# Condition products of tiles 12 to 29 as seven block products a pair

## What is computed

```python
masked_w = weight * mask[None]                       # 8 x 512 x 512
w_bot = einsum('bg,got->bot', y, masked_w)           # one 512 x 512 matrix a batch
h = einsum('bnt,bot->bno', x, w_bot) + bias          # the condition products
gate = silu(bitlinear(h, w_gate)); up = bitlinear(h, w_up)
out = x + bitlinear(gate * up, w_down)
# bitlinear(a, w): a is rounded to 8 bits by its row's largest absolute value,
# w to -1, 0, 1 times the mean of its absolute values
```

## Time and profile before

| | us |
|---|---|
| median of 3 runs | 455.29 |
| lowest, highest | 454.59, 455.42 |
| the profiled execution | 456.14 |
| its span from the first to the last instruction | 454.3 |
| PE busy in it | 436.5 |
| DVE, ACT, POOL busy | 366.3, 326.9, 154.4 |

### The profile page before, as it was taken

The page is one execution under the profiler, slowest core; times in us unless marked ns, Lnnn a source line. Parts: engine busy times, 40 slices in busy tenths (PEclk is TensorE's granted clock), DMA queues, the critical chain, the costliest instruction groups (busy, mean ns, idle before and its releaser), DMA issues.

```text
span 454.3 us, 7179 instructions
## 1 busy us (share of the span) xinstructions
PE 436.5 (96%) x2170; PEld 231.7 (51%) x2170; DVE 366.3 (81%) x624; ACT 326.9 (72%) x448; POOL 154.4 (34%) x160
## 2 busy tenths in 40 slices
PE   4899998999999999999999999999999999999976
PEld 0234443444444455555565556555565555655543
DVE  0316579898956798799998999999999899999971
ACT  1216847785356786988888888888888888888951
POOL 0000170606099554141424414244142432423202
PEclk9999999999999999999999999999999999999989
DMA  7999996995420335253544535344263552635454
GB/s 281 403 399 415 413 249 152 335 278 129 93 48 19 74 71 138 73 115 93 142 81 129 115 83 147 74 135 115 76 155 69 137 119 69 162 66 135 80 139 139
DMA packets 104313, 69.78 MB, mean 154 GB/s; under 512 B 87264, under 2 KB 87264, under 8 KB 102752
## 3 DMA queue, kind: packets, MB, share of 16 engines
q1 hardware_dynamic: 103712, 67.39, 53.8%
q10 hardware_dynamic: 576, 2.10, 1.3%
HBM read 40.11 MB, written 8.39 MB: 107 GB/s over the span
## 4 chain that ended last, share of the span: by engine, by line
PE 77%; DMA 12%; DVE 4%; ACT 3%; issue 2%; SPq 1%; ACTq 0%; DVEq 0%
PE ps L882 24%; PE ps L945 19%; PE ps L917 17%; PE ps L837 10%; DMA wc<-w_gate 4%; PE ps L875 4%; DMA qT<-q_sb 3%; DMA wc<-wcond 2%; DMA wc<-w_down 2%; PE ps L952 2%; PE ps L850 1%; ACT tern_up L406 1%; ACT h_sb L412 1%; DMA wc<-wc 1%; DVE h_max L658 1%
## 5 line engine op out<-in xcount | busy, mean ns | idle before, releaser
L882 PE MATMUL ps<-tern_up,qT 128*128 128x512 f16 x512 | 131.3, 379 | 0.6 <-DVE wc L728 0.6
L837 PE MATMUL ps<-w_bot,xT_sb 128*128 128x512 f32 x256 | 113.2, 595 | 2.3 <-DVE w_bot L633 1.6
L746 DVE TENSOR_REDUCE p_part<-wc 128x1 f32<-128x1536 f32 x64 | 77.9, 1217 | 1.7
L837 PEld LDWEIGHTS ps<-w_bot,xT_sb 128*128 128x128 f32 x256 | 48.0, 190 | 61.2 <-issue 57.5
L882 PEld LDWEIGHTS ps<-tern_up,qT 128*128 (+1 forms) x512 | 50.0, 98 | 55.3 <-DVE wc L728 1.3
L728 DVE TENSOR_TENSOR wc<-ps,xT_sb 128x512 f32<-128x512 f32 x104 | 71.2, 684 | 7.6 <-issue 3.6
L470 ACT ACTIVATE wc<-wc 128x1024 f16<-128x1024 f32 x64 | 66.9, 1051 | 1.8 <-DMA wc<-wc 1.3
L460 ACT ACTIVATE wc<-wc,p_scale 128x2048 f32<-128x2048 f32 x31 | 62.1, 2002 | 4.4 <-DVE p_scale L784 4.4
L945 PE MATMUL ps<-wc 128*128 128x256 f16 x480 | 62.2, 273 | 0.2 <-DVE wc L696 0.2
L696 DVE TENSOR_TENSOR wc<-wc 128x1024 f16<-128x1024 f16 x60 | 56.8, 946 | 3.7 <-DMA wc<-wc 2.5
L455 ACT ACTIVATE xT_sb<-ps,gate_unit 128x512 f32<-128x512 f32 x78 | 49.2, 683 | 11.7 <-PE ps L917 11.3
(11 more groups left out here) (91 smaller groups left out, 544.4 us busy)
## 6 DMA issues: line engine op xcount, KB each, us to landing
xT_sb<-xT SPq DMA_DIRECT2D x32, 256.0 KB, 7.7
x_res<-x SPq DMA_DIRECT2D x30, 256.0 KB, 2.9
out<-result SPq DMA_DIRECT2D x30, 256.0 KB, 2.4
wc<-wcond SPq DMA_DIRECT2D x12, 512.0 KB, 13.7
wc<-w_gate SPq DMA_DIRECT2D x4, 1024.0 KB, 17.7
wc<-w_up SPq DMA_DIRECT2D x4, 1024.0 KB, 13.4
wc<-w_down SPq DMA_DIRECT2D x4, 1024.0 KB, 7.3
wc<-wcond ACTq DMA_DIRECT2D x4, 512.0 KB, 7.6
```

Of the source, the lines that this page charges most:

```text
L746: nc.vector.tensor_reduce(p_part[:, par, i:i + 1], prod[:, par, 512 * lo:512 * hi], AX.X, ALU.max, apply_absolute_value=True).then_inc(par ...
L837: ins = nc.tensor.matmul(ps[:, t % COND_BANKS], xT_sb[:, t % XSLOTS, k], w_bot[:, t // HALF, k], start=(k == 0), stop=(k == KH - 1))
L882: ins = nc.tensor.matmul(ps[:, UP + i % 2], tile_of(s, k), tern_up[:, i, k], start=(k == 0), stop=(k == KH - 1))
```

## The change

- The tiles 12 to 29 become nine pairs r = 6 to 14 (PAIR0 to PAIR_END - 1). Each pair's 2 x 2 output blocks are made by seven products of two k-blocks by 256 columns (pair_product) instead of eight. POOL forms four sums of the tiles' blocks a pair (pair_sum) and, once a batch, four combinations of w_bot's blocks (combine_cond).
- The banks of a pair are 2 (r % 3) and the one after; bank 6 holds the shared block. ACT writes half the bias into a bank ahead of the products (seed_bias) and copies the first product over (copy_first). DVE has pair_share, pair_seed and pair_c22, which add into PSUM, and one pair_largest for both tiles. ACT rounds straight from the bank (pair_round). There is no bias add for these tiles.
- PE's order puts the products 4, 5 and 6 of a pair between those of the next; the last pair's stand beside the first two gate chunks of step 0. Tiles 8 to 11 now use banks 2 to 5. The sums of absolute values stand before tile 9 and in pairs 8 and 12.
- ACT issues the loads of the gate and up weights itself, behind its copies of w_bot and between its first tiles; SP's list of loads is rearranged and the down weight's pieces come with transposes 8 to 11. The x_res loads follow the last transpose.
- The mask of batch 1 moves from DVE to POOL. POOL scales each weight piece between the sums, and DVE cuts a piece as soon as that one is scaled. The last two pieces of the down weight are cut inside step 0. combine_gate(1) follows unit_of(1) and combine_gate(0) follows unit_of(2).
- At the end ACT converts half 0 of tile 30 before copy_seed, SP stores tile 26 before the transposes of tile 30, and tile 31's down products are cut into two halves of 256 columns with a bank, a finish and a store each (down_cut).

The diff, cut to its core (the new functions as far as they carry the order):

```diff
+PLAIN = 12
+PAIR0 = PLAIN // 2
+PAIR_END = LATE // 2
+COND_C = 6
+SUM_TILE = 9
+SUM_PAIR = {8: 1, 12: 2}
+SUM_BANK = (5, 7, 7)
...
+            for t in range(XSLOTS, PLAIN):
+                load_xT(t)
+            transpose_q(0)
+            for t in range(PLAIN, PLAIN + 2):
+                load_xT(t)
+            for k in range(KH):
+                load_mask(1, k)
+            for t in range(1, PAIR0):
                 transpose_q(t)
+                load_xT(PLAIN + 1 + t)
+            for t in range(PAIR0, PLAIN):
+                transpose_q(t)
+                if t == PAIR0:
+                    load_xT(PLAIN + 1 + t)
+                if t >= PLAIN - PIECES:
+                    sp.wait_ge(tern_done, t - PLAIN + PIECES + 1)
+                    load_raw(2, w_down, t - PLAIN + PIECES)
+            for r in range(PAIR0, PAIR_END):
+                for t in (2 * r, 2 * r + 1):
+                    transpose_q(t)
+                for t in (2 * r, 2 * r + 1):
+                    if t + XSLOTS < TILES:
+                        load_xT(t + XSLOTS)
...
+                    pool.wait_ge(x_sum_ready, 4 * n + (0, 1, 0, 2)[i])
+                in0, in1, op = ((a21, a22, ALU.add), (sums[:, 0], a11, ALU.subtract), (a11, a21, ALU.subtract),
+                                (a12, sums[:, 1], ALU.subtract))[i]
+                nc.gpsimd.tensor_tensor(sums[:, i], in0, in1, op).then_inc(x_sum_ready, 1)
...
+            combine_cond(0)
+            for k in range(KH):
+                apply_mask(k)
+            scale_piece(0, 0)
+            scale_piece(0, 1)
+            first_sums(6)
+            last_sums(6)
+            scale_piece(0, 2)
+            scale_piece(0, 3)
+            first_sums(7)
+            last_sums(7)
+            combine_cond(1)
+            first_sums(8)
+            last_sums(8)
+            first_sums(9)
+            scale_piece(1, 0)
+            last_sums(9)
+            scale_piece(1, 1)
+            first_sums(10)
+            scale_piece(1, 2)
+            last_sums(10)
+            scale_piece(1, 3)
+            for r in range(11, 14):
+                first_sums(r)
+                last_sums(r)
+            scale_piece(2, 0)
+            first_sums(14)
+            scale_piece(2, 1)
+            last_sums(14)
+            scale_piece(2, 2)
+            scale_piece(2, 3)
...
+            def seed_bias(r):
+                bank = pair_banks(r)[1]
+                if r < PAIR0 + 3:
+                    act.wait_ge(h_ready, (2, 10, 12)[r - PAIR0])
+                    act.wait_ge(s_bias, 16)
+                else:
+                    act.wait_ge(h_rounded, 2 * r - 5)
+                nc.scalar.activation(ps[:, bank, 0:NB], bias_sb[:, 0:NB], ACT.Copy).then_inc(cond_seeded, 1)
+
+            def copy_first(r):
+                b0, b1 = pair_banks(r)
+                act.wait_ge(cond_first, r - PAIR0 + 1)
+                if r >= PAIR0 + 3:
+                    act.wait_ge(h_rounded, 2 * r - 4)
+                nc.scalar.activation(ps[:, b0, 0:NB], ps[:, b1, 0:NB], ACT.Copy).then_inc(cond_copied, 1)
...
@@ -538,10 +682,10 @@
                     if j is not None:
                         copy_seed(j)
                 else:
+                    if s == TILES - 1:
+                        convert(s - 1, 0, 0)
                     copy_seed(j)
-                    convert(s - 1, 0, 0)
-                if s == TILES - 1:
-                    convert(s - 1, 0, 1)
...
+            for a in range(PIECES):
+                fetch(0, w_gate, a)
+            act.wait_ge(mix_psum, 2 * KH)
             for a in range(PIECES):
                 abs_sum_piece(0, a)
...
+            for a in range(PIECES - 1):
+                cond_round(PIECES + a)
+                abs_sum_piece(1, a)
+            cond_round(7)
+            copy_first(PAIR0)
+            seed_bias(PAIR0 + 1)
+            abs_sum_piece(1, 3)
+            cond_round(8)
+            cond_round(9)
+            copy_first(PAIR0 + 1)
+            cond_round(10)
+            cond_round(11)
+            seed_bias(PAIR0 + 2)
+            for r in range(PAIR0 + 2, PAIR_END):
+                copy_first(r)
+                pair_round(r - 2, 1)
+                if r + 1 < PAIR_END:
+                    seed_bias(r + 1)
+                pair_round(r - 2, 0)
+                pair_convert(r - 2)
+                if 8 <= r < 8 + PIECES:
+                    abs_sum_piece(2, r - 8)
+            pair_round(PAIR_END - 2, 1)
...
                 n = PIECES * m + a
-                dve.wait_ge(scaled, PIECES * (m + 1))
...
+            def pair_share(r):
+                dve.wait_ge(bias_diff_ready, 1)
+                dve.wait_ge(cond_shared, r - PAIR0 + 1)
+                nc.vector.tensor_tensor(pair_shared(r), ps[:, COND_C, 0:NB], bias_diff[:, :], ALU.add
+                                        ).then_inc(cond_shared_out, 1)
+
+            def pair_seed(r):
+                b0, b1 = pair_banks(r)
+                dve.wait_ge(cond_u2, r - PAIR0 + 1)
+                dve.wait_ge(cond_shared_out, r - PAIR0 + 1)
+                nc.vector.tensor_tensor(ps[:, b0, NB:HID], ps[:, b1, 0:NB], pair_shared(r), ALU.add).then_inc(cond_summed, 1)
+
+            def pair_c22(r):
+                b1 = pair_banks(r)[1]
+                dve.wait_ge(cond_u3, r - PAIR0 + 1)
+                dve.wait_ge(cond_shared_out, r - PAIR0 + 1)
+                nc.vector.tensor_tensor(ps[:, b1, NB:HID], ps[:, b1, 0:NB], pair_shared(r), ALU.add).then_inc(cond_c22, 1)
+
+            def pair_largest(r):
+                b0, c = pair_banks(r)[0], 4 + 2 * (r % 2)
+                dve.wait_ge(cond_psum, 2 * r + 2)
+                if r >= PAIR0 + 2:
+                    dve.wait_ge(h_rounded, 2 * r - 2)
...
+            bias_difference()
+            piece_after = {7: 0, 8: 1, 10: 2}
+            for t in range(PLAIN):
                 cond_tile(t)
+                if t == 5:
+                    weight_mean(0)
                 if t in piece_after:
+                    ternary_piece(0, piece_after[t])
+            for r in range(PAIR0, PAIR_END):
+                if r > PAIR0:
+                    pair_seed(r - 1)
+                if r >= PAIR0 + 2:
+                    pair_largest(r - 2)
+                pair_share(r)
+                if r > PAIR0:
+                    pair_c22(r - 1)
+                if r == PAIR0:
+                    ternary_piece(0, 3)
+                if r == 8:
+                    weight_mean(1)
+                if r == 9:
                     units(0)
+                if 10 <= r < 10 + PIECES:
+                    ternary_piece(1, r - 10)
+                if r == 12:
+                    weight_mean(2)
+                if r == 14:
+                    ternary_piece(2, 0)
+            pair_seed(PAIR_END - 1)
+            pair_largest(PAIR_END - 2)
+            pair_c22(PAIR_END - 1)
+            ternary_piece(2, 1)
+            pair_largest(PAIR_END - 1)
...
+                         ps[:, b0, NB:HID], ps[:, b1, 0:NB])[i]
+                for k in range(2):
+                    tile, weight = ((sums[:, 0, k], combos[:, 0, k]), (xT_sb[:, s0, k], w[:, k, 0:NB]),
+                                    (xT_sb[:, s0, 2 + k], w[:, 2 + k, 0:NB]), (sums[:, 1, k], combos[:, 1, k]),
+                                    (sums[:, 2, k], combos[:, 2, k]), (sums[:, 3, k], w[:, 2 + k, NB:HID]),
...
                     pe.wait_ge(half_merged, 2 * KH)
                 else:
+                    pe.wait_ge(h_ready, cond_bank(t) + 1)
...
+                pair_product(r, 1)
+                pair_product(r, 0)
+                if r in SUM_PAIR:
+                    abs_total(SUM_PAIR[r])
+                if r > PAIR0:
+                    pair_product(r - 1, 4)
+                    pair_product(r - 1, 5)
+                pair_product(r, 2)
+                pair_product(r, 3)
+                if r > PAIR0:
+                    pair_product(r - 1, 6)
 
             for s in range(3):
```

318 lines of the change are left out of this document (222 added, 96 removed).

## The result

The changed kernel takes 476.09 us (median of 4 runs, 475.58 to 476.77) beside 454.94 us (454.27 to 455.42) of the kernel before on the same chip: a ratio of 1.0464, 95% interval 1.0434 to 1.0494. It is slower by 21 us; 451.6 was predicted, at most 457. The profiled execution has a span of 473.9 us (454.3 before) and a mean granted clock of 0.970.

A forecast was written before the change was run, and what follows sets the result against it. PE, busy for 96% of the span, was taken to bound the kernel. Stage -0.5 and end -3.2, with nothing between, make -3.7 us: 451.6 us from the median of 455.3, range 448.0 to 457.0.

The forecast's parts named there:

- stage: Condition products before the gate chunks at 128.92 us: -4.0 + 1.7 + 1.8 = -0.5 us.
- middle: Between 129 and 430 us: costed at nothing, uncertain by 1 us each way.
- end: Tiles 30 and 31: earlier conversion, shorter transpose wait without the clock falling, smaller last store; -3.2 us, from -1.5 to -4.
- Pair products: Nine pairs of tiles: 28 records of 0.217 us instead of 16 of 0.430, 0.81 less a pair, 7.3 us in all.
- The rival of narrow products that don't halve: Pair products at 0.24 instead of 0.217 us a record: 252 records cost 5.8 us more, 457.4 us; chance 0.08.
- The ramp, 53 to 80 us: Start of the pairs, where the gain was expected to be spent: PE waits leave 4.0 us of gain before two further costs.
- ACT is a queue: In the ramp ACT works in order through pieces, tiles and DMA issues: copy for pair 6 at 67.2, PE waiting 0.7 us.
- 65 us of work in 87: POOL's masks, combinations, sums and scalings from about 37 to 124 us, taken to keep up with PE.
- DVE and POOL together: Eight ternary instructions before the seed of pair 6, slowed by a busy POOL: 0 to 3.4 us, 1.7 taken.
- The clock: PE's idle of 3.2 + 1.7 us in the ramp is followed by the lower clock: 1.8 us (0 to 3.5).
- The port lock in full: Rival: ternary pieces at 60 to 80 us each wait for a POOL instruction, 1 to 1.5 us; 456.3 us, chance 0.25.
- the 4.0 us of the prediction: Gain of the condition stage without further cost: gate chunks at 124.9 instead of 128.92 us.

The follow-up runs named there:

- e1: The changed kernel with batch 1's masks issued on SyncE's queue behind the last condition weight: 469.86 us (1.0313 to the kernel before).
- g4: e1 with the loads of w_gate and w_up left out, all work on them running on what lies in the buffers: 460.61 us (1.0119).
- p1: g4 with GpSimd's scaling of w_gate and w_up left out as well: 456.52 us (1.0037).
- e3: The changed kernel with both weights back on SyncE's queue in the order of the kernel before, which also brings the masks forward: 469.16 us (1.0295).
- f1: e1 with w_up's four pieces fetched one each behind ScalarE's tiles 4 to 7: 465.89 us (1.0224).
- g3: e1 with the load of w_up left out, the work on it running on what lies in its buffer: 460.87 us (1.013).
- e2: The changed kernel with GpSimd applying the same late masks behind the sums of pair 7: 471.02 us (1.0349).
- p2: The kernel before with TensorE, from tile 12 on, made to wait for VectorE's read of a more recent tile: 463.06 us (1.0165).
- h2: The kernel before with GpSimd's combinations of w_gate in the changed kernel's order: 459.41 us (1.009).
- e4: The kernel before with only the change's orders at the end (tile 30's conversion, tile 26's store, tile 31 in halves): 452.25 us (0.995).
- f4: The changed kernel with w_up's pieces fetched behind tiles 4 to 7, masks where the change has them: 469.83 us (1.0357).

## Why the prediction was wrong

The sum was: stage -0.5, middle 0, end -3.2. Measured in the profiled execution: +15.5, +3.3, +0.8. By the three marks, each kernel's one profiled execution against that of the kernel before (us):

| kernel | stage | steps 0 to 5 | rest |
|---|---|---|---|
| changed | +15.5 | +3.3 | +0.8 |
| e1, masks early | +11.9 | +3.3 | -1.0 |
| g4, besides without the two loads | +3.6 | +3.3 | -2.0 |
| p1, besides without the scaling | -1.8 | +3.3 | -1.9 |

Point by point:

- **Pair products, -7.3: right.** 0.216 us a record against 0.217. The rival of narrow products that don't halve has fallen.
- **The ramp, 53 to 80 us: the step that failed**, in four of its terms. The prediction's queue has PE wait 1.1, 0.7, 3.2 and 1.5 us, 6.5 in all; measured are 18.3. (The 1.1 us before the first sum didn't come: it runs at 52.99 without a wait. And the second wait counts as 1.5 us in the queue, but as 1.7 where the clock is costed.)
  - "ACT is a queue" without the landing of its transposes. The wait of 7.1 us before the convert of tile 4 stood in the trace of before, and the prediction didn't look at it, because no one waited for ScalarE there. That transposes off the weights' ring help ScalarE is hardly so: its convert of tile 4 starts at 60.49 in the changed kernel and at 62.85 before, but at 62.20 in e1 and at 61.99 with the weights back on that ring (e3). f1, g3 and g4 give the transfers 4 to 9 us, all of it by w_up's.
  - POOL's masks were counted as load (65 us of work in 87), not by landing. GpSimd could start them at 62.88 only, and they held the first scaling and the first block sums, for which PE stood 8.93 us: 5 to 6 us of the time (e1, e2). For POOL's sums the prediction had no wait at all.
  - DVE and POOL together, "0 to 3.4, I take 1.7": the eight instructions took 13.8 instead of 7.6 us. p1 shows what the stretching is worth in the time, 4 us.
  - The clock, "1.8 (0 to 3.5)": 6.5 us. Three idle times of 8.93, 2.38 and 5.29 us follow one another within 25 us, and the granted clock is 0.85, 0.64 and 0.53 in the three windows of 60 to 90 us.
- **What covers.** The prediction asked of each new wait what product covers it, but not what the old banks had covered. p2 is the measure: with three tiles instead of eight the kernel before loses 8 us by what it has always had on its other engines. I take this for the root, since the pairs leave PE about a pair ahead. For the kernel before it is shown; for the changed one it is argued, as no run gives the lead back there.
- **The port lock in full** was the rival with the right sign (456.3). The page named with it ("SBUF — State Buffer", section "SBUF: two separate sides", in the Trainium skill) agrees with these rows: after, a ternary instruction of 1.21 us takes 2.99 beside GpSimd, whose scaling ends at 71.7, that is 1.1 us before the instruction does, and in h2 two additions of 0.70 take 4.93. But the eight were not all stretched alike (1.09 to 2.99 us each), and the price was taken for the ramp alone and by itself.
- **Middle, 0 +- 1:** +3.3. The combinations of w_gate were not costed where they now lie, beside VectorE's additions of steps 3 to 5 (h2: 3.9 us). Of w_down's combinations the prediction asked only when they are wanted, not what runs beside them.
- **End, -3.2:** -2.3 by itself (e4). In the changed kernel it gave nothing in the profiled execution: the idle time before 458.32 is 2.10 us, since the transpose took 4.7 us to land (3.2 in e4), and the clock was at the lower level for the 5.31 us. e1's, e2's and e3's profiles have the same idle time of 2.0 to 2.1 us, e2's with the lower clock behind it, e1's and e3's with the full one; g4 and p1 (1.90 us, full clock) gain 1.9 to 2.0 in the rest. So the idle time takes part of the gain, and the clock the other part in some executions only. Why the landing is longer in the kernels with pairs from tile 12 stays open. The 1.8 us that the prediction put on the clock there are not sure either: in p2 an idle time of 2.31 us at this place has the full clock behind it.

By medians: 476.1, with masks early 469.9, without the two loads 460.6, without the scaling 456.5. What is left over 454.9 is less than the 3.3 us of steps 0 to 5, and the stage is then 1.8 us shorter than before. That is less than the 4.0 us of the prediction, since 3.95 us of idle time before the shared block remain. g4 and p1 leave work out and are no kernels to use; I could not make a whole kernel with pairs that beats the kernel before, and the best version measured is e4.

## What to carry to other kernels

A change that takes work from the bounding engine and buffers with it must be costed by the lead that it takes away: list each wait of the other engines in the trace of before, also those that nobody waited for, and ask which of them come through with the lead that is left. Of each transfer in an in-order queue ask when it lands under the load that the change makes, not how much work hangs on it. Where GpSimd gets work, look for VectorE's fast instructions on its path at that very time, in stages far behind the change as well.

## What the runs showed of the hardware

- An issue on SyncE's queue can itself be held back while another queue's transfers are on their way: the four masks took 2.5 to 3.1 us each to issue from 44.8 us on in the changed kernel, and 0.44 to 0.65 at the same place and time with w_up's loads later (f4). One transpose took 9.0 us to issue in e1.
- A 128 x 512 transpose, 2.5 us by the median of the changed kernel, landed 18.1 us after its issue at 42.3 us, although w_gate and w_up were in another queue.
- GpSimd's float16 subtractions stretch VectorE's float16 additions of 128 x 1024 from 0.70 to 2.5 us each.
- Behind one idle time of 6.45 us the granted clock is 0.81 from 80 to 90 us (p2); behind three in 25 us it is 0.53 there (after).
- The same idle time of 2.0 to 2.3 us at the end of the kernel is followed by the lower clock in some executions (before, after, e2: 16 products take 5.31 us) and by the full one in others (e1, e3, p2: 3.63 us).
